# Transposes of xbc one block later, last taps ahead of dt's polynomial, second group's first input products inside the first MLP's first block

## The reference

```
h0 = layernorm(x)
r  = rmsnorm(h0) * ln1
z, xs, B, C, dt = split(r @ w_in.T)              # 512, 128, 128, 512, 4 columns
xs, B, C = silu(conv4(concat(xs, B, C)) + conv_b)  # causal, 4 taps, per channel
dt = softplus(dt + dt_bias);  a = dt * -exp(A_log)
y  = state-space scan of xs, B, C, dt, a in chunks of 128 tokens, 4 heads, + D * xs
h1 = h0 + (y * silu(z)) @ w_out.T
h2 = h1 + mlp(rmsnorm(h1) * ln2)                 # gate, up: 1792; silu(gate) * up; down
x1 = x + layernorm(h2)
n  = layernorm(x1)
out = x1 + layernorm(n @ W_up.T + the rank-8 LoRA product of the expert with the largest logit)
```

## Time and profile before

| | |
|---|---|
| time of 3 runs, median (lowest, highest) | 840.18 us (839.14, 840.97) |
| the profiled execution's own time | 837.98 us |
| its span, first to last instruction | 836.1 us |
| PE busy | 770.9 us (92%) |
| DVE, ACT, POOL busy | 478.1, 331.5, 150.0 us |
| mean granted clock of TensorE | 0.965 |

### The profile page before, as it was taken

How to read it: one execution, slowest core, us unless ns; L and a number is a source line. 1 busy time by engine, 2 the same in 40 slices (tenths; PEclk the granted TensorE clock), 3 DMA queues, 4 the chain that set the end, 5 groups by cost and what they waited for, 6 DMA issues and landing times.

```text
span 836.1 us, 13857 instructions
## 1 busy us (share of the span) xinstructions
PE 770.9 (92%) x5558; PEld 540.1 (65%) x5558; DVE 478.1 (57%) x1109; ACT 331.5 (40%) x603; POOL 150.0 (18%) x197
## 2 busy tenths in 40 slices
PE   4994989999999999999999999999999999999945
PEld 3853856676657866586666866677666866577632
DVE  6874667875635665475645565465644564265163
ACT  2642676625423443324523453325523353222211
POOL 1420121214110331014110331014110320010010
PEclk9995999999999999999999999999999999999987
DMA  9931000300104020210104020210103110021010
GB/s 331 387 131 26 1 26 1 67 11 26 26 2 97 5 51 1 52 52 26 26 1 78 25 51 1 51 51 21 33 1 63 39 27 1 11 66 27 1 50 26
DMA packets 59936, 41.11 MB, mean 49 GB/s; under 512 B 45664, under 2 KB 45792, under 8 KB 59872
## 3 DMA queue, kind: packets, MB, share of 16 engines
q1 hardware_dynamic: 59872, 40.22, 17.4%
HBM read 25.01 MB, written 4.19 MB: 35 GB/s over the span
## 4 chain that ended last, share of the span: by engine, by line
PE 80%; DVE 10%; ACT 4%; issue 2%; DMA 2%; SPq 1%; POOL 0%; POOLq 0%; DVEq 0%; ACTq 0%
PE gu L1252 32%; PE wa L1252 22%; PE acc L1252 17%; PE wc L1252 7%; DVE xbc L944 2%; DVE weights L871 2%; ACT L621 1%; DMA weights<-in_w_in 1%; ACT silu_z L614 1%; DVE sg L1044 0%; DVE stats_c L886 0%; DVE dts L970 0%; PE wa L1340 0%; DVE h L1074 0%; DMA xa<-in_x 0%
## 5 line engine op out<-in xcount | busy, mean ns | idle before, releaser
L1252 PE MATMUL gu<-h2t,weights 128*128 128x256 f16 x2688 | 320.2, 277 | 0.0
L1252 PEld LDWEIGHTS gu<-h2t,weights 128*128 128x128 f16 x2688 | 264.5, 99 | 58.4 <-issue 19.7
L1252 PE MATMUL acc<-weights,act 128*128 128x512 f16 x672 | 163.4, 379 | 5.8 <-DVE act L1049 5.8
L1044 DVE SCALAR_TENSOR_TENSOR sg<-gu,bound,sg 128x256 f32<-128x256 f32 x112 | 53.7, 480 | 136.9 <-ACT sg L670 136.8
L670 ACT ACTIVATE sg<-gu,scale_inv 128x256 f32<-128x256 f32 x112 | 52.9, 472 | 172.9 <-PE gu L1252 172.8
L1252 PE MATMUL wa<-ht,weights 128*128 128x256 f16 x912 | 110.3, 280 | 5.3 <-DMA ht<-ra 5.3
L1252 PEld LDWEIGHTS wa<-ht,weights 128*128 128x128 f16 x912 | 91.4, 100 | 23.9 <-DMA ht<-ra 5.7
L1252 PEld LDWEIGHTS acc<-weights,act 128*128 128x128 f16 x672 | 65.3, 98 | 63.2 <-DVE act L1049 7.9
L680 ACT ACTIVATE act<-sg 128x256 f16<-128x256 f32 x112 | 46.6, 416 | 98.4 <-DVE sg L1044 97.6
L1049 DVE TENSOR_TENSOR act<-sg,act 128x256 f16<-128x256 f32 x112 | 52.0, 464 | 54.0 <-ACT act L680 54.0
L944 DVE SCALAR_TENSOR_TENSOR xbc<-wa,conv_ws,xbc 128x253 f32<-128x253 f32 (+1 forms) x132 | 57.3, 475 | 3.0 <-ACT xbc L597 1.5
(11 more groups left out here) (194 smaller groups left out, 790.4 us busy)
## 6 DMA issues: line engine op xcount, KB each, us to landing
xa<-in_x SPq DMA_DIRECT2D x8, 512.0 KB, 3.5
weights<-in_x SPq DMA_DIRECT2D x8, 512.0 KB, 3.7
out_x<-h SPq DMA_DIRECT2D x16, 256.0 KB, 2.2
weights<-in_w_in SPq DMA_DIRECT2D x5, 512.0 KB, 6.5
weights<-in_w_down SPq DMA_DIRECT2D x3, 768.0 KB, 13.2
weights<-in_w_gate SPq DMA_DIRECT2D x2, 1024.0 KB, 12.7
weights<-in_w_up SPq DMA_DIRECT2D x2, 1024.0 KB, 14.1
weights<-in_w_gate SPq DMA_DIRECT2D x2, 768.0 KB, 14.3
```

Source lines behind the costliest of these rows:

```text
L1044: nc.vector.scalar_tensor_tensor(sg[:, f % 2], GU[f % 2][:, SEQ:2 * SEQ], up_to_act, sg[:, f % 2], ALU.mult, ALU.mult).then_inc(sem("prod_ ...
L1252: return nc.tensor.matmul(dst, left, right, start=start, stop=stop)
```

## The change

In every step, PE's `a_tok` moves from the end of block 3 to the head of block 4's A part, before `a_dec(0)`, `a_dec(1)`, and so behind gu(4) and down(3). ACT's `a_tok` moves with it, from the end of block 3 to behind `b_silu(4)` and `b_hi(4)`, before `a_exp`. On DVE, in block 2, the taps of the last channel pair (`a_conv(g, 2)`) come before dt's polynomial (`a_dt`).

At the prologue's end, PE's `a_in(1, 0)` and ACT's `a_conv(1, 0)` leave `first()` and stand in step 1's block 0, behind gu(0) (for ACT behind `prepare(0)`, `b_silu(0)` and `b_hi(0)`). ACT's `a_t2(0)` comes before `a_hi1(1)`, and DVE's `a_t2(0)` before three `lower_halves` and `a_lo1(1)`.

```
--- before.py
+++ after.py
@@ -702,10 +702,10 @@
                 eng.wait_ge(sem("u_ps_ready"), g * 2 + j + 1)
                 nc.scalar.activation(h3[:, j], u_bank(g, j)[:], ACT.Copy, scale=inv_lin).then_inc(sem("u_ready"), 1)
 
-            A_AT = {0: lambda g: a_conv(g, 1), 1: lambda g: (a_conv(g, 2), a_silu(g, 0)),
+            A_AT = {0: lambda g: (g == 1 and a_conv(g, 0), a_conv(g, 1)), 1: lambda g: (a_conv(g, 2), a_silu(g, 0)),
                     2: lambda g: (a_silu(g, 1), a_z(g, 0), a_dt(g)),
-                    3: lambda g: (a_silu(g, 2), a_z(g, 1), a_tok(g)),
-                    4: lambda g: (a_exp(g, 0), a_exp(g, 1)), 6: lambda g: (a_exp(g, 2), a_state(g)),
+                    3: lambda g: (a_silu(g, 2), a_z(g, 1)),
+                    4: lambda g: (a_tok(g), a_exp(g, 0), a_exp(g, 1)), 6: lambda g: (a_exp(g, 2), a_state(g)),
                     8: lambda g: a_sumsq(g, 0), 9: lambda g: a_sumsq(g, 1), 11: lambda g: a_hi2(g)}
             NEXT_AT = {10: lambda g: a_hi1(g), 13: lambda g: a_conv(g, 0)}
             C_AT = {4: lambda g: (c_t3(g, 0), c_t3(g, 1)) if alone(g) else c_hi3(g), 7: lambda g: c_zt(g),
@@ -755,9 +755,8 @@
                 a_sumsq(0, 0)
                 a_sumsq(0, 1)
                 upper_halves(range(S_GU + 7, S_MIX))
+                a_t2(0)
                 a_hi1(1)
-                a_t2(0)
-                a_conv(1, 0)
                 chain_a.close()
 
             first()
@@ -1151,7 +1150,7 @@
                     nc.vector.tensor_tensor(h3[:, j], h3[:, j], x1[:, j], ALU.add).then_inc(sem("out_ready"), 1)
 
             A_AT = {0: lambda g: a_conv(g, 0), 1: lambda g: (a_conv(g, 1), a_dtv(g)),
-                    2: lambda g: (a_dt(g), a_conv(g, 2)), 3: lambda g: a_h0(g),
+                    2: lambda g: (a_conv(g, 2), a_dt(g)), 3: lambda g: a_h0(g),
                     5: lambda g: (a_dec(g, 0), a_dec(g, 1), a_att(g, 0)), 6: lambda g: a_att(g, 1),
                     7: lambda g: (a_y(g, 0), a_y(g, 1)), 8: lambda g: a_h1(g, 0),
                     9: lambda g: a_h1(g, 1), 10: lambda g: a_weight(g), 11: lambda g: a_lo2(g)}
@@ -1492,8 +1491,8 @@
                     c_linear(g, j)
                 c_lora(g, j)
 
-            A_AT = {0: lambda g: a_in(g, 1), 1: lambda g: (a_in(g, 2), a_dt(g)), 2: lambda g: a_z(g, 0),
-                    3: lambda g: (a_z(g, 1), a_tok(g)), 4: lambda g: (a_dec(g, 0), a_dec(g, 1)),
+            A_AT = {0: lambda g: (g == 1 and a_in(g, 0), a_in(g, 1)), 1: lambda g: (a_in(g, 2), a_dt(g)), 2: lambda g: a_z(g, 0),
+                    3: lambda g: a_z(g, 1), 4: lambda g: (a_tok(g), a_dec(g, 0), a_dec(g, 1)),
                     5: lambda g: (a_att(g, 0), a_dec(g, 2)), 6: lambda g: (a_att(g, 1), a_state(g)),
                     7: lambda g: (a_y(g, 0), a_y(g, 1)), 8: lambda g: a_o(g, 0), 9: lambda g: a_o(g, 1)}
             NEXT_AT = {13: lambda g: a_in(g, 0)}
@@ -1555,7 +1554,6 @@
                 a_o(0, 1)
                 spread(2)
                 a_t2(0)
-                a_in(1, 0)
 
             first()
             steps(step)
```

## The result

| | before | after |
|---|---|---|
| median of runs (lowest, highest) | 839.66 us (835.96, 840.97), 4 runs | 815.67 us (815.18, 817.58), 4 runs |
| profiled execution, its span | 837.98 us, 836.1 | 815.18 us, 813.3 |
| PE busy | 770.9 us (92%) | 762.6 us (94%) |
| mean granted clock | 0.965 | 0.975 |

The ratio is 0.9725, 95% interval 0.969 to 0.9761. The chain that ended last is now 85% PE, before 80%.

What follows compares the result with a forecast made beforehand. PE's queue was taken to bound the kernel. Gains of 13.5 + 8.3 + 3.3 - 1.0 = 24.1 us took the profiled 837.98 to 813.9; adding half of the 2.2 us median gap gave 815.0, range 811 to 822.

Steps and rivals of the forecast that it cites:

- The wait and its reason: Ahead of `a_tok`'s transposes, PE loses 2.25 us per step to DVE's order; taps first hide in DVE's 5.65 us idle.
- Transposes later, `tok` later: In blocks 3 and 4, moving PE's transposes and ACT's copy costs and gains nothing, with 2.0 us left for ACT.
- Steps 2 to 7: Six steps without the 2.25 us wait give 13.5 us, and five avoided clock falls 8.3 us.
- The clock: Behind the transposes' wait, PE's clock falls cost 1.66 us each; five vanish with the idle, 8.3 us gained.
- Step 1, the term that was mis-sized: At step 1's transposes and down(3), waits shrink by 2.24 + 1.06 = 3.3 us; bounds 1.5 and 4.
- The rival that the rule was used for: `b_lo(3)` held up by POOL, down(3) 1.45 us late in each of 6 steps: 8.7 us back, 823.7; chance 0.08.
- The start of step 1: Up to gu(1), the second group's rows land later by DMA, a loss of 1.0 us; bounds 1.7 gain, 3.7 loss.
- The net of step 1: Over step 1, a 3.3 us gain from shorter PE waits less a 1.0 us loss at its start.
- The median: Whole kernel: 813.9 us for the profiled execution, plus half the 2.2 us by which the median exceeded it, 815.0.

Runs made afterwards that it cites:

- the first experiment: The kernel before with only DVE's taps of the last channel pair put ahead of dt's polynomial, transposes left in place: 814.38 us, ratio 0.9728.
- 4 dummies: The changed kernel with 4 unread DVE instructions between the last taps and dt's polynomial in every step: 815.24 us, ratio 0.9722.
- 8 dummies: The changed kernel with 8 unread DVE instructions between the last taps and dt's polynomial in every step: 828.98 us, ratio 0.9887.

## Why the prediction was right

The forecast was 815.0 us in 811 to 822; measured 815.67. By its steps:

**The wait and its reason.** Right. DVE's order alone takes it away; the taps end 3.04 us before the polynomial (forecast 3.0), and the polynomial does not move. The cover is that size: 2.86 us of other work fit in, 5.75 do not.

**Transposes later, `tok` later.** Right that they bring "no gain, no loss" in steps 2 to 7: without them, in the first experiment, these steps take the same time. Alone they move the wait to down(3). The prediction did not say what the change would give without them; by the first experiment, as much.

**Steps 2 to 7.** 13.5 + 8.3 = 21.8 us forecast. The trace has 660.1 - 637.8 = 22.3. A step with a fall gave 95.13 - 91.21 = 3.92, the one without 2.26; with five of the former that is 21.9. The rest of 0.4 lies in the last 20 us, which the change doesn't touch: the products `acc<-weights,h3t` took 4.47 us there before and 4.02 after. One effect was left out and cost nothing: `b_lo(3)` now being early, DVE's next two instructions, which make `h` from `xa`, run beside POOL's `ra` and `tdt` and take 2.44 us for 0.99, and POOL's two pairs take 2.22 and 2.40 us for 2.04.

**The clock.** The saving of 1.66 per fall is right, and that none is left in steps 2 to 7. That a fall is tied to the idle ahead of it is right as well, but not each idle brings one: 2.1 us brought it in five of seven cases in one trace and in three of seven in another. By the extremes of all runs the kernel before moved between 834.1 and 841.0 us, the changed one between 814.5 and 817.6. That fits seven chances of 1.66 us that are gone, but the executions without a trace don't show where their clock fell.

**Step 1, the term that was mis-sized.** Forecast: "Gain 2.24 + 1.06 = 3.3", from a wait at down(3) of 0.35 us. It measured 2.51. Three weight halves were put in at 2.07 us and took 3.63; the lower half was put in at 0.42 and took 1.30. Both ran beside POOL's `ra` and `tdt`. In the kernel before, the same three halves at this place took longer too; the text took their duration from another place:

```profile
108.81 2.49 POOL L461 TENSOR_TENSOR hn<-tri,dts 128x512 f32<-128x512 f32 x2
109.24 3.27 DVE L871 SCALAR_TENSOR_TENSOR weights<-weights,scale_v 128x512 f16<-128x512 f32 x3
```

The Trainium skill's rule on the shared port ("SBUF — State Buffer", "Who interferes with whom") was weighed for `b_lo` only. Its wording, a VectorE instruction with two SBUF inputs, covers the weight halves as well, which read both their inputs from SBUF; the trace agrees, 2.06 us without POOL and 3.63 beside it. In the other direction the sum left out a gain: the wait of 0.58 us that stood at down(5) of step 1 before is gone. Behind gu(1), step 1 gained 88.96 - 87.15 = 1.8 us of the 3.3 forecast. The rival that the rule was used for, `b_lo(3)` held up until PE waits, did not come in steps 2 to 7: `b_lo(3)` took 0.53 us there and ended 1.7 us before it was needed.

**The start of step 1.** Forecast: a loss of 1.0 us up to gu(1). Measured: 88.37 - 69.81 = 18.56 us, before 87.02 - 69.30 = 17.72, so 0.84. The wait of 3.71 us and the 8.06 of both pairs of input products (forecast: 3 us or more, and 5.3 + 2.62 = 7.9) are as forecast. The start alone loses 0.94 over the whole of step 1, and splitting the second group's rows first shortens the same distance by 3.85: the late DMA is the cause. The net of step 1, forecast 2.3, measured 0.97 in the distances.

**The median.** Sum against the profiled execution: 813.9 forecast, 815.18 measured; the difference is step 1's 1.3 us and a prologue longer by 0.5, less steps 2 to 7's 0.5. The half of the 2.2 us between profile and median that was added made up for half of it: 1.1 us had been added, and the gap measured 0.5. That the forecast is off by no more than 0.7 us is partly luck, since these two misses, 1.3 and 0.6, lie in opposite directions.

## What to carry to other kernels

When the engine that sets the end waits for another one again and again, look first at what that other engine does in the wait's shadow: here 2.7 us of ready work stood behind a wait of 5.65 us for something else, and exchanging two entries of a table was worth some 22 us, the whole gain of the change. Test the smallest part of a change alone before building the rest. Price an instruction by a row of the same instruction beside the same neighbours on GpSimd, not by its fastest row. And when work is put into a hole ahead of a transfer, check what its own producers push back: the hole was filled, but the transfer started 3.4 us later, and giving its rows back their place brought some 815.6 down to 810.5 us.

## What the runs showed of the hardware

How long PE sat idle did not alone decide whether TensorE's clock fell from its higher level (2.4 GHz) to the lower (1.2 GHz) behind the idle. Idles of 2.1 us were followed by a granted clock of 0.66 over 5 us in five of seven steps of one trace and in three of seven of another. The wait of 2.5 us at down(3) of step 1 was followed by a fall in two of four traces; one of 2.8 us (with 4 dummies) and even one of 3.86 us (transposes' place alone) by none; behind one of 5.7 us (with 8 dummies) it fell. After the six waits of 1.17 us there was none. What decides it, the runs don't show.

VectorE instructions with two SBUF inputs took longer beside GpSimd work: `b_lo(3)` 0.53, 0.93 and 1.30 us for 0.42, and three weight halves 3.27 and 3.63 us for 2.06. GpSimd's pair of `ra` took 2.92 instead of 2.04 us beside the weight halves. One tensor from SBUF, with two per-partition scalars, was enough too:

```profile
290.38 2.44 DVE L919 TENSOR_SCALAR h<-xa,mv_a,small_a 128x512 f32<-128x512 f32 x2
291.32 2.40 POOL L461 TENSOR_TENSOR hn<-tri,dts 128x512 f32<-128x512 f32 x2
```

Before, where the first row came behind GpSimd's work, it took 0.99 us, in each of steps 2 to 7. The taps, with one input in PSUM, took 2.67 to 2.69 us for six, also beside GpSimd.
